# First pass of a two-pass graph kernel: GpSimd waits for a gather to land before every twelfth one

## What is computed

```
x = x + gnn0(layernorm(x))      # gather feat[src], sum by dst, two 256x256 products, leaky relu, normalise
x = x + layernorm(x) @ Wf.T + bf
x = x + gnn1(layernorm(x))      # gather h[src], times relation_emb[type], gate, sum by dst, products
x = x + ffn(layernorm(x))       # half of the nodes, chosen by score, 256 -> 1024 -> 256
```

## Time and profile before

| what | us |
|---|---|
| median of three runs (lowest, highest) | 5625.84 (5616.38, 5627.58) |
| the profiled execution, its own time | 5668.76 |
| its span, first to last instruction | 5666.6 |
| set-up, up to the first gather of the first pass | 247.7 |
| first pass, first gather to last summed slot | 2556.3 |
| between the passes | 27.4 |
| second pass, first gather to last summed slot | 2762.2 |
| rest | 73.4 |

### The profile page before, as it was taken

One profiled execution on the slowest core, in us unless ns is written; L12 is line 12 of the kernel. 1 busy time (PEld: TensorE's weight loads), 2 busy tenths in 40 slices (PEclk: granted clock), 3 DMA queues, 4 the chain that ended last, 5 costly groups with the idle time before them and its releaser, 6 DMA issues.

```text
span 5666.6 us, 69897 instructions
## 1 busy us (share of the span) xinstructions
PE 3878.1 (68%) x20836; PEld 2999.7 (53%) x20836; DVE 2898.9 (51%) x11712; ACT 1601.5 (28%) x6319; POOL 3285.2 (58%) x3447
## 2 busy tenths in 40 slices
PE   6555645555555565555568878788888887888786
PEld 6444434443444444444446666666666665666565
DVE  8755545555545555555544444444444444444445
ACT  3054445444545444444300111111011110110111
POOL 0166666666666666666466665555555655555552
PEclk9577777777777777777789898899899998988898
DMA  4333333333333333333244444444444444434443
GB/s 95 120 91 97 95 95 96 97 98 95 97 94 95 96 95 95 93 96 97 80 125 110 110 107 105 105 106 105 105 105 105 109 106 102 109 101 107 103 107 85
DMA packets 275015, 571.57 MB, mean 101 GB/s; under 512 B 86332, under 2 KB 164377, under 8 KB 274643
## 3 DMA queue, kind: packets, MB, share of 16 engines
q0 software_dynamic: 164640, 456.82, 32.3%
q1 hardware_dynamic: 98162, 101.78, 5.8%
q10 hardware_dynamic: 11840, 8.50, 0.5%
HBM read 539.92 MB, written 26.92 MB: 100 GB/s over the span
## 4 chain that ended last, share of the span: by engine, by line
PE 40%; DVE 31%; another core or an unknown queue 19%; issue 8%; DMA 1%; ACT 0%; DVEq 0%; SPq 0%; PEldq 0%; ACTq 0%
PE psE L732 16%; PE psT L714 6%; PE psY L714 6%; DVE both L1355 5%; DVE accf L1429 5%; DVE accf L1425 4%; PE psE L899 3%; PE psE L918 3%; DVE accf L1355 2%; DVE work L1261 2%; PE psE L853 1%; PE psY L677 1%; DVE work L1372 1%; PE psE L803 1%
## 5 line engine op out<-in xcount | busy, mean ns | idle before, releaser
L614 POOL DMA_INDIRECT work<-t_d,srci x3430 | 3277.4, 956 | 2297.3 <-issue 1273.7
L732 PE MATMUL psE<-work,both 128*128 128x257 f32 x5152 | 1648.3, 428 | 442.5 <-DVE work L1372 216.4
L1087 ACT ACTIVATE accf<-accf,work 128x35 f16<-128x35 bf16 x5145 | 1150.9, 311 | 1242.5 <-DVE accf L1425 800.0
L732 PEld LDWEIGHTS psE<-work,both 128*128 128x128 f32 x5152 | 962.6, 215 | 638.8 <-issue 333.6
L1425 DVE TENSOR_SCALAR accf<-iob,work 128x35 bf16<-128x35 bf16 x1715 | 275.2, 255 | 944.8 <-remote 746.6
L1372 DVE TENSOR_TENSOR work<-work,psT 128x257 f32<-128x257 f32 x858 | 345.7, 419 | 719.6 <-remote 227.1
L1372 DVE TENSOR_TENSOR work<-work,psY 128x257 f32<-128x257 f32 x857 | 345.4, 419 | 706.5 <-PE psY L714 260.2
L1355 DVE TENSOR_SCALAR both<-iof,dstf 128x128 f32<-128x128 f32 x2576 | 550.8, 297 | 43.3 <-remote 22.6
L714 PE MATMUL psT<-relb,work 125*128 125x257 bf16 x3381 | 554.5, 288 | 22.8 <-DVE work L1363 16.5
L714 PE MATMUL psY<-relb,work 125*128 125x257 bf16 x3381 | 550.8, 286 | 13.3 <-issue 12.9
L732 PE MATMUL psE<-work,accf 128*128 128x257 f32 x1708 | 483.4, 439 | 42.7 <-issue 40.9
(11 more groups left out here) (276 smaller groups left out, 3565.0 us busy)
## 6 DMA issues: line engine op xcount, KB each, us to landing
work<-t_d,srci POOLq DMA_INDIRECT x3430
work<-types_d SPq DMA_DIRECT2D x245, 218.8 KB
both<-acc_d SPq DMA_DIRECT2D x98, 130.0 KB
t_d<-accf SPq DMA_DIRECT2D x7, 910.0 KB, 9.1
acc_d<-work ACTq DMA_DIRECT2D x1, 6370.0 KB
t_d<-accf SPq DMA_DIRECT2D x49, 130.0 KB
X<-in_x SPq DMA_DIRECT2D x1, 6144.0 KB
out<-X SPq DMA_DIRECT2D x6, 896.0 KB
```

The costliest lines, as they stand in the source:

```text
L614: pool.indirect_dma_start((gath if layer else gath0)[:, k, :], None, table, bass.IndirectOffsetOnAxis(ap=srci[:, n:n + 1], axis=0)).then_i ...
L732: ins = nc.tensor.matmul(psE[:, b % 2, 0:DW], picks(layer, n // SG)[:, k % SG, :], (gath if layer else gath0)[:, ring(layer, n), 0:DW], st ...
L1087: ins = nc.scalar.activation(to_s3[:, n % SENDS, i, j, :], to_s[:, n % SENDS, i, :], ACT.Copy, scale=load3[:, b // RB % 2, j, w:w + 1])
```

## The change

In the first pass only, before gather n where n is 12, 24, 36 up to 1704, GpSimd now waits until gather n-1 has landed. That is 142 waits. The wait for the ring's free place stays as it is, behind the new one. Nothing else changes: no instruction of another engine, no size and no order. Where both waits stand, the gather starts when both are fulfilled. Gathers n+1 to n+11 stand behind gather n in GpSimd's queue.

```
+BURST = 12
...
             def gathers(layer, table):
                 for n in range(SLOTS):
                     k = ring(layer, n)
+                    if layer == 0 and n > 0 and n % BURST == 0:
+                        pool.wait_ge(s_g[ring(layer, n - 1)], 16 * loads(layer, n - 1))
                     if n >= (RG if layer else RG0):
                         pool.wait_ge(s_mm, summed(layer * SLOTS + n - (RG if layer else RG0) + 1))
                     pool.indirect_dma_start((gath if layer else gath0)[:, k, :], None, table, bass.IndirectOffsetOnAxis(
                         ap=srci[:, n:n + 1], axis=0)).then_inc(s_g[k], 16)
```

## The result

| | kernel before | changed kernel |
|---|---|---|
| median of 12 runs each, us | 5625.44 (5605.16 to 5646.64) | 5645.35 (5622.88 to 5664.49) |
| ratio, 95% interval | 1 | 1.0038 (1.0021 to 1.0054) |
| the profiled execution, its own time | 5668.76 | 5622.88 |
| its first pass, first gather to last sum | 2556.3 | 2531.2 |
| its second pass | 2762.2 | 2741.0 |

The change makes the kernel 20 us slower. The forecast was 51 us faster; 5645 us lies inside the range that was given, but on the other side of no change. So the two profiles, laid side by side, say the opposite of the twelve runs. They can show how the pass is built, but not where 20 us went.

What follows compares the result with a forecast made beforehand. The prediction took the first pass to be bound by GpSimd's loop of gather bursts and pauses, with PE's counts held during bursts. +112 - 96 - 67 = -51 us took 5625.8 to 5575 us, range 5512 to 5700.

Steps and rivals of the forecast that it cites:

- The reading: First pass: PE's counts reach other engines late while GpSimd issues gathers, and come through when it pauses.
- First term, added pauses: GpSimd, first pass: 60 multiples of 12 without a pause get one, 1.9 us each, +112 us.
- Second term, odd pauses that vanish: GpSimd, first pass: 37 of 70 pauses at odd multiples of 6 go away, -96 us.
- Third term: First pass: DVE's waits end up to 328 us earlier; about half of GpSimd's 133 us pause time goes, -67 us.
- The first, the balance: First pass: freed consumers do not use the gain, GpSimd makes up the rest in pauses; +16 us, 5615 to 5637, chance 0.16.
- The second: First pass: 2.2 us pauses end before counts come through, the 37 odd pauses stay; +112 us, 5738, chance 0.31.
- The third, a lock between VectorE and GpSimd: First pass: L1425 waits for GpSimd itself to get at SBUF, not for counts; 5738 us, chance 0.04.

Runs made afterwards that it cites:

- burst6: Changed kernel with the forced wait before every sixth gather instead of every twelfth (285 waits): 5803.01 us, 1.0224.
- a clearing alone: One small GpSimd memset before each twelfth gather, in place of the changed kernel's landing wait: 4732.46 us, 1.0044, where no counts are held.
- the wait with one clearing: Changed kernel plus one small GpSimd memset behind each forced wait: 5587.46 us, 0.9927 where counts are held; 5030.21 us, 1.0685 where not.

## Why the prediction was wrong

**What bounds the kernel.** The reading held: counts of TensorE are held back while GpSimd issues gather after gather, and they come through in its pauses. The share of counts let through by length of pause shows it, burst6 too (747 us of waits for nobody down to 9), and the kernel before where nothing is held shows how much hangs on it: 960 us between the two profiles, 376 of them in the first pass and 588 in the second, which I took as given.

**First term, added pauses, +112 us.** The forced pause, where nothing prolongs it, is 2.1 us where I took 2.2, so 60 x 1.8 = 108. Held.

**Second term, odd pauses that vanish, -96 us.** 33 were to be left; 31, 31 and 22 are, with no burst of 18 and 164 to 173 pauses in all against some 175 forecast. Held. The odd ones sum to 131 to 165 us less than before, about as much as the forecast had for this term and the odd pauses' share of the next together (96 and 43).

**Third term, -67 us given back on top: this is the step that failed.** It had VectorE's held waits shrink by 328 us, which the 142 letting-through pauses were to end. They went from 853 and 878 us to 834, 838 and 838, and L1429's waits for nobody to 774 where 500 or less was forecast. In the working, the choice that was wrong is the pause taken at 2.2 us as if any pause let the counts through. Two rows had said otherwise: 2.4 and 3.3 us from the last issue to the count. Pauses below 2.25 us let 76 of 171 through. Therefore the 81 pauses that stood at multiples of 12 before did not shrink from 2.75 towards 2.2: 25 to 30 of the forced ones became 3.0 to 3.5 us, as at 529.94 above, the landing first and then the held `s_mm`. The 142 sum to 358, 383 and 382 us, where all at 2.2 would be 312. The sum of all pauses was to be 375 us and is 417, 458 and 425 (before: 428, 431). On average that is 58 us above the forecast, out of the 71 between 51 faster and 20 slower.

**The sum.** Without the third term my working gives +16 us; 20 were measured. I don't take this as proof: the profiles spread by 49 us, and the sum of the pauses moved by +4 on average, so the 20 us themselves are not found in the pauses.

**The rivals.** The first, the balance, has the price of +16 us, and what was measured lies just above its band. The second names the mechanism, a pause of 2.2 us that ends before the counts are through and decides at about 2.4 us; it erred in that the 37 odd pauses do vanish all the same, so that the loss is 20 us and not 112. Its point of decision is borne out: with 2.6 us per pause, 0.5 more than the changed kernel's, the time is 41 us below before. That this is near the 51 forecast for the change itself is partly luck, since the forecast had shorter pauses. The third, a lock between VectorE and GpSimd on their way to SBUF, falls: where no count is held, the same VectorE instructions beside the same stream of gathers never wait for nobody. The Trainium skill, "SBUF — State Buffer", "Who interferes with whom", states such a lock for VectorE's 2-port modes; no run here shows it at these instructions.

**Open.** Why the wait for gather n-5, which never pauses, costs 0.34% where counts are held. Since it does, part or all of the changed kernel's 0.38% may come from the instruction of the wait and not from the pauses; what the pauses show is why the gain did not come. Whether a clearing alone, without the landing wait, does good there: it ran only where nothing is held. The gain of 0.73% was measured on one chip, in six runs, and the kernel before has no profile from that chip. And why one chip holds the counts and another doesn't: nothing in the kernel decides it, and no experiment of mine reached it.

## What to carry to other kernels

When a wait is given to an engine as a remedy for something that its pauses cure, work out first how long a pause must be for the cure, from the rows where a pause did and did not help, and set the wait's length against it: here 2.1 us cost 0.38%, 2.6 gained 0.73%, 2.9 gained nothing. Measure the length that comes out, too: mine was taken from an average and was 0.1 us off. What an engine waits on a late count is worth no more than the loop behind it allows: here VectorE's 747 us could be taken to 9 while the kernel grew 2.2% slower. And a gain that rests on waits for nobody is a gain on the chips that show such waits; look at more than one before taking it.

## What the runs showed of the hardware

- The same kernel took 5625 to 5677 us on some chips and 4708 to 4718 on others. What differs in the traces is when semaphore counts arrive: TensorE's come 13 to 15 ns behind the matmul on the latter. On the former they come several us late, up to 24.5 before a start of VectorE, and only in the passes of gathers. GpSimd's own cadence is 1.26 us a gather on both.
- Not only TensorE's counts are late there. Of the recorded arrivals of ScalarE's count behind L1087 52% are over 0.3 us late, of VectorE's behind L1355 38% (first profile of the kernel before; none on the other chips). What waits for these loses little: TensorE's `move` starts at most 11 us late by them in the whole first pass.
- With runs of six gathers at most (7.5 us) VectorE has 8.8 us of waits for nobody; with runs of up to twelve, 774 us.
- GpSimd goes on 2.06 us behind the end of the issue of a gather of 133 KB (128 rows of 1040 bytes) when it waits for its landing, 3.0 us from the issue's start (473.48 to 476.48 in the rows above), and 0.9 us when it waits for the gather before that one.
- By the Trainium skill, "DMA: Bandwidth & Descriptors", section "Anatomy of one DMA — SWDGE (gpsimd) path", a DMA takes about 2.0 us and the time of its bytes. For these bytes that makes 0.31 us and 2.3 in all, an estimate by the page's rate; the rows have 3.0 from the issue's start to GpSimd's next gather.
- Profiles of one kernel differ by 49 us in the first pass alone where counts are held, and by 4 us where they are not (2502, 2499 and 2500 us for the wait with one clearing).
